# Earlier gathers in the inputs of layer 0 with the norm on ScalarE, 16384 bytes for descriptors, and a register read one tile ahead

## What is computed

```python
def mixture(x):                       # per token: the two best experts of the gate
    w = softmax(top2(x @ Wg + bg + bias))
    return sum(w[k] * (relu(x @ W1[e[k]] + b1[e[k]]) @ W2[e[k]] + b2[e[k]]) for k in (0, 1))

x = x + mixture(layernorm(x))         # its sum is taken in the attention inputs of layer 0
h = layernorm(x)
q, k, v = rope(h @ Wq + bq), rope(h @ Wk + bk), h @ Wv + bv
```

## Time and profile before

| | us |
|---|---|
| median of three runs | 2529.16 (2523.53 to 2530.19) |
| the profiled execution | 2531.16, its span 2529.3 |
| expert tiles, layer 0 | about 451 to 568 |
| attention inputs, layer 0 | about 570 to 720 |
| attention inputs, layer 1 | about 1403 to 1480 |
| expert tiles, layer 1 | about 2277 to 2412 |
| closing stage | about 2412 to 2529 |

### The profile page before, as it was taken

The page is one execution under the profiler, slowest core; times in us unless marked ns, Lnnn a source line. Parts: engine busy times, 40 slices in busy tenths (PEclk is TensorE's granted clock), DMA queues, the critical chain, the costliest instruction groups (busy, mean ns, idle before and its releaser), DMA issues. The chain is left out here.

```text
span 2529.3 us, 45491 instructions
## 1 busy us (share of the span) xinstructions
PE 2030.4 (80%) x16896; PEld 958.9 (38%) x16896; DVE 1988.9 (79%) x3319; ACT 1507.4 (60%) x2948; POOL 593.3 (23%) x702
## 2 busy tenths in 40 slices
PE   6999675882479999999999579999999999369910
PEld 4888464771222222222222322222222222359910
DVE  7887647565679999999994779999999994576635
ACT  5553330340118988989888218988989889105500
POOL 2444300667520000000000340000000000316555
PEclk9999885895769999999999769999999999559955
DMA  5000010243341010110100351010110100302211
GB/s 192 1 1 1 0 32 11 78 91 78 115 147 32 20 42 19 33 42 20 42 6 10 110 153 31 21 42 19 32 42 20 42 6 10 122 10 74 64 51 55
DMA packets 94411, 121.16 MB, mean 48 GB/s; under 512 B 23664, under 2 KB 56560, under 8 KB 93936
## 3 DMA queue, kind: packets, MB, share of 16 engines
q1 hardware_dynamic: 73712, 78.92, 11.3%
q0 software_dynamic: 8960, 18.37, 3.0%
q10 hardware_dynamic: 11520, 20.98, 2.7%
HBM read 69.70 MB, written 42.99 MB: 45 GB/s over the span
## 5 line engine op out<-in xcount | busy, mean ns | idle before, releaser
L1489 DVE TENSOR_REDUCE mx<-psum 128x1 f32<-128x1024 f32 x1024 | 1175.1, 1216 | 82.2 <-PE psum L1377 81.3
L1466 ACT ACTIVATE p<-psum 128x512 f32<-128x512 f32 x2048 | 1102.5, 596 | 108.8 <-PE psum L1399 66.2
L1411 PE MATMUL psum<-p,v_ext 128*32 128x256 f32 x8192 | 656.5, 392 | 39.3 <-ACT p L1466 39.2
L1377 PE MATMUL psum<-ks,qs 64*128 64x512 bf16 x2048 | 636.0, 395 | 53.1 <-DVE mx L1489 29.9
L1399 PE MATMUL psum<-qs,ks 64*128 64x512 bf16 x2048 | 630.6, 383 | 1.5 <-ACT p L1466 1.3
L1411 PEld LDWEIGHTS psum<-p,v_ext 128*32 128x32 f32 x8192 | 162.2, 108 | 474.2 <-ACT p L1466 254.6
L1279 POOL CAST m_near<-mx 128x16 bf16<-128x16 f32 x128 | 25.1, 196 | 1080.9 <-DVE mx L1489 1076.8
L1399 PEld LDWEIGHTS psum<-qs,ks 64*128 64x128 bf16 x2048 | 123.4, 93 | 404.0 <-ACT p L1466 368.0
L746 ACT ACTIVATE hid<-psum,stage 128x128 f32<-128x128 f32 x448 | 132.1, 366 | 180.3 <-PE psum L716 180.3
L690 POOL DMA_INDIRECT x_in<-n_rows,token_of x152 | 166.2, 1093 | 296.3 <-POOLq L85 229.2
L1377 PEld LDWEIGHTS psum<-ks,qs 64*128 64x128 bf16 x2048 | 118.7, 94 | 115.3 <-DVE mx L1489 81.3
(11 more groups left out here) (229 smaller groups left out, 2120.7 us busy)
## 6 DMA issues: line engine op xcount, KB each, us to landing
qs<-qk_parts SPq DMA_DIRECT2D x128, 104.0 KB
ks<-qk_parts SPq DMA_DIRECT2D x128, 104.0 KB
qk_parts<-piece__1 ACTq DMA_DIRECT2D x40, 256.0 KB, 3.7
qk_parts<-piece__2 ACTq DMA_DIRECT2D x40, 256.0 KB, 3.5
answers<-y_out SPq DMA_DIRECT2D x152, 64.0 KB, 1.5
ew<-in_moe SPq DMA_DIRECT2D x1, 5136.0 KB, 18.8
ew<-in_moe SPq DMA_DIRECT2D x1, 4624.0 KB, 13.9
n_rows<-n_all SPq DMA_DIRECT2D x8, 512.0 KB, 3.2
```

The costliest lines, as they stand in the source:

```text
L1377: pe.matmul(psum[:, bank, :], a["qs"][r, g % NKF, j % KM, i * P:(i + 1) * P], a["ks"][r, g % NKF, j % KM, k * HALF:(k + 1) * HALF], start= ...
L1411: last = pe.matmul(psum[GR * j:GR * j + VW, O_BANK, q], t["v_ext"][:, b * NT + i, VE * (h0 + j):VE * (h0 + j) + VW], a["p"][:, (GH * s + j ...
L1466: act.activation(a["p"][:, n % NP, :], psum[:, S_BANK + n % NS, :], ACT.Exp, scale=DH ** -0.5)\
L1489: dve.tensor_reduce(a["mx"][:, g % 2, h, j, 0, c:c + 1], psum[:, bank:bank + 2, :].rearrange("p a c -> p (a c)"), AX.X, ALU.max)\
```

## The change

Four things. In the attention inputs of layer 0, batch 1 is normalised after batch 0 has been rotated; GpSimd issues all 64 gathers first, each batch behind the wait for its place, and the rests of batches 0 and 1 move to VectorE, each one job behind its rotation. In the attention inputs of both layers the eight tile operations of the norm move from VectorE to ScalarE, which applies x times rstd plus a shift; VectorE computes the shift in one small operation. The memory for descriptors is 16384 bytes. In the expert tiles of both layers the register with the expert's number is read one tile ahead, behind the stage copy before.

```diff
@@ expert_tiles, VectorE
-            def stage_weights(i):
-                e = dve.value_load(t["expert_of"][0:1, i:i + 1], min_val=0, max_val=t["E"] - 1)
+            def find_expert(i):
+                return dve.value_load(t["expert_of"][0:1, i:i + 1], min_val=0, max_val=t["E"] - 1)
+
+            def stage_weights(i, e):
                 if i >= NST:
                     dve.wait_ge(y_ready, i - NST + 1)
                 dve.tensor_copy(t["stage"][:, i % NST, :], t["ew"][:, bass.ds(e, 1), :]
                                 .rearrange("p a c -> p (a c)")).then_inc(staged, 1)
-            stage_weights(0)
+            stage_weights(0, find_expert(0))
+            e = find_expert(1)
             for i in range(tiles + 2):
...
                 if i + 1 < tiles:
-                    stage_weights(i + 1)
+                    stage_weights(i + 1, e)
+                    if i + 2 < tiles:
+                        e = find_expert(i + 2)
@@ attention_inputs
+    def after(b):
+        return layer == 0 and b == 1
+
+    def rested_by_vector(b):
+        return layer == 0 and b < 2
@@ TensorE
-                if b + 1 < B:
+                if b + 1 < B and not after(b + 1):
                     turn(b + 1)
                 project(b, (1,))
                 values(b)
+                if after(b + 1):
+                    turn(b + 1)
+        def take_rest(eng, n):
...
+            eng.wait_ge(piece0, n + 1)
+            if n >= RESTS:
+                eng.wait_ge(piece2, n - RESTS + 1)
+            eng.tensor_tensor(a["rest"][:, n % RESTS, :], a["rot"][:, n % ROTS, :],
+                              a["pieces"][0][:, pair % PAIRS, c], ALU.subtract).then_inc(rest, 1)
@@ VectorE, norm(b)
-                norm_steps(dve, t, link, (var_ready, std_ready, tile_ready), b, a["x"][b](), a["norm"][b]())
...
+                dve.scalar_tensor_tensor(t["shift"][:, 0, :], t["mv"][:, :, 0], -1.0, rstd, ALU.mult, ALU.mult)\
+                    .then_inc(scales_ready, 1)
@@ VectorE, rotate(b)
+                    if rested_by_vector(b) and n > JB * b:
+                        take_rest(dve, n - 1)
                     if layer == 0 and n >= LATE:
                         last_piece(dve, n - LATE)
...
+                if rested_by_vector(b):
+                    take_rest(dve, JB * (b + 1) - 1)
...
-                if b + 1 < B:
+                if b + 1 < B and not after(b + 1):
                     norm(b + 1)
                 rotate(b)
+                if after(b + 1):
+                    norm(b + 1)
@@ GpSimd
             if layer == 0:
-                for b in range(2):
+                for b in range(B):
+                    if b >= 2:
+                        pool.wait_ge(mixed, 2 * NT * (b - 1))
                     fetch(pool, t, b)
-            for b in range(B):
-                if layer == 0 and b + 2 < B:
-                    pool.wait_ge(mixed, 2 * NT * (b + 1))
-                    fetch(pool, t, b + 2)
-                take_rest(b)
+            for n in range(len(jobs)):
+                if not rested_by_vector(n // JB):
+                    take_rest(pool, n)
+                if layer and n >= LATE:
+                    last_piece(pool, n - LATE)
@@ ScalarE, copy_turned(b), behind the root
+                act.wait_ge(scales_ready, b + 1)
+                for i in range(NT):
+                    act.activation(a["norm"][b](i, 1).rearrange("p a d -> p (a d)"),
+                                   a["x"][b](i, 1).rearrange("p a d -> p (a d)"), ACT.Identity,
+                                   scale=t["rstd"][:, 0, i:i + 1], bias=t["shift"][:, 0, i:i + 1]).then_inc(tile_ready, 1)
@@ ScalarE, the order of batches
-                if b + 1 < B:
+                if b + 1 < B and not after(b + 1):
                     copy_turned(b + 1)
                 for n in range(JB * b, JB * (b + 1)):
                     first_piece(n)
-                    if n:
+                    if n and not (n == JB and after(1)):
                         second_piece(n - 1)
+                if after(b + 1):
+                    second_piece(JB * (b + 1) - 1)
+                    copy_turned(b + 1)
@@ kernel
-    nc = bacc.Bacc("TRN2", target_bir_lowering=False, num_devices=1, dynamic_dma_scratch_size=2048)
+    nc = bacc.Bacc("TRN2", target_bir_lowering=False, num_devices=1, dynamic_dma_scratch_size=16384)
```

More of the change, by code:

```diff
@@ L997, in attention_inputs @@
     T_BANK, V_BANK = 6, 4
-    with stage(nc, "loaded", "row_set", "rows_stored", "mixed", "step", "var_ready", "std_ready", "tile_ready", "turned",
+    def after(b):
+        return layer == 0 and b == 1
+    def rested_by_vector(b):
+        return layer == 0 and b < 2
+    with stage(nc, "loaded", "row_set", "rows_stored", "mixed", "step", "var_ready", "std_ready", "scales_ready", "tile_ready", "turned",
                "y_copied", "proj_done", "rot_a", "rot_used", "summed", "piece0", "rest", "piece1", "piece2", "v_done", "v_used", "cleared") as \
-            (block, loaded, row_set, rows_stored, mixed, step, var_ready, std_ready, tile_ready, turned,
+            (block, loaded, row_set, rows_stored, mixed, step, var_ready, std_ready, scales_ready, tile_ready, turned,
              y_copied, proj_done, rot_a, rot_used, summed, piece0, rest, piece1, piece2, v_done, v_used, cleared):
@@ L1071, in _ @@
                 values(b)
+                if after(b + 1):
+                    turn(b + 1)
+        def take_rest(eng, n):
+            b, k, h = jobs[n]
+            c, pair = slice(h * HALF, (h + 1) * HALF), 2 * b + k
+            eng.wait_ge(piece0, n + 1)
[3 more added lines that the diff above has]
+                              a["pieces"][0][:, pair % PAIRS, c], ALU.subtract).then_inc(rest, 1)
         def last_piece(eng, n):
@@ L1087, in norm @@
                     combine(dve, t, b, mixed, a["x"][b], a["x"][b], 2 * NT * b)
-                norm_steps(dve, t, link, (var_ready, std_ready, tile_ready), b, a["x"][b](), a["norm"][b]())
+                var, std, rstd, tmp = (t[k][:, 0, :] for k in ("var", "std", "rstd", "tmp"))
+                for i in range(NT):
+                    last = dve.bn_stats(t["stats"][:, i, :], a["x"][b](i, 1).rearrange("p a d -> p (a d)"))
+                link(last)
+                for i in range(NT):
+                    last = dve.bn_aggr(t["mv"][:, i, :], t["stats"][:, i, :])
+                link(last)
+                dve.tensor_scalar(var, t["mv"][:, :, 1], EPS, None, ALU.add).then_inc(var_ready, 1)
+                dve.wait_ge(std_ready, b + 1)
+                link(dve.reciprocal(rstd, std))
+                link(dve.tensor_tensor(tmp, rstd, rstd, ALU.mult))
+                link(dve.tensor_tensor(tmp, tmp, var, ALU.mult))
+                link(dve.tensor_scalar(tmp, tmp, -0.5, 1.5, ALU.mult, ALU.add))
+                link(dve.tensor_tensor(rstd, rstd, tmp, ALU.mult))
+                dve.scalar_tensor_tensor(t["shift"][:, 0, :], t["mv"][:, :, 0], -1.0, rstd, ALU.mult, ALU.mult)\
+                    .then_inc(scales_ready, 1)
             def rotate(b):
@@ L1139, in _ @@
         def _(pool):
-            def take_rest(b):
-                for n in range(JB * b, JB * (b + 1)):
-                    _, k, h = jobs[n]
-                    c, pair = slice(h * HALF, (h + 1) * HALF), 2 * b + k
-                    pool.wait_ge(piece0, n + 1)
-                    if n >= RESTS:
-                        pool.wait_ge(piece2, n - RESTS + 1)
-                    pool.tensor_tensor(a["rest"][:, n % RESTS, :], a["rot"][:, n % ROTS, :],
-                                       a["pieces"][0][:, pair % PAIRS, c], ALU.subtract).then_inc(rest, 1)
-                    if layer and n >= LATE:
-                        last_piece(pool, n - LATE)
             if layer == 0:
-                for b in range(2):
+                for b in range(B):
+                    if b >= 2:
+                        pool.wait_ge(mixed, 2 * NT * (b - 1))
                     fetch(pool, t, b)
-            for b in range(B):
-                if layer == 0 and b + 2 < B:
-                    pool.wait_ge(mixed, 2 * NT * (b + 1))
-                    fetch(pool, t, b + 2)
-                take_rest(b)
+            for n in range(len(jobs)):
[3 more added lines that the diff above has]
+                    last_piece(pool, n - LATE)
             if layer:
```

## The result

The changed kernel takes 2498.39 us (median of 4 runs, 2496.07 to 2502.17) against 2529.64 for the kernel before: a ratio of 0.9886, 95% interval 0.9873 to 0.9898, or -31 us. Forecast were 2495.2 in a range of 2485 to 2510.

The account below looks back on a forecast made before the run. Bounds were seen in GpSimd's gathers, stalled by descriptor room and order, and VectorE's register load in layer-0 tiles; -7.5 - 17 - 8 - 0.5 - 1 = -34 us gave 2495.2, range 2485 to 2510.

Parts of the forecast that it names:

- Closing stage, -7.5: Closing stage: with more descriptor room, four holes between the 64 gathers, together 7.5 us, go; 0 if they have another cause.
- 112 gathers: Descriptor room: if 2048 bytes hold 14 gathers, 16384 hold some 112, more than the run of 64.
- Layer-0 inputs, -17: Attention inputs of layer 0: with the new order the last combine starts at 662.5, not 679.40, so -17 us.
- Rival D: Layer-0 inputs: VectorE's two-operand work holds nearly every gather, +35 us, 2564 in all; chance 0.04.
- Layer-0 tiles, -8: Expert tiles of layer 0: the early register read brings a tile to 1.30 us, so -8 us.
- if x waits for it, 0.34 comes back: 2.6, 1.30: Layer-0 tiles: if the moved read holds the next x copy, two tiles take 2.6 us, 1.30 each.
- rival C: Layer-0 tiles: the load's idle time only moves, tiles stay at 1.35; -26 us in all, 2503; chance 0.10.
- 2.5 landing + 3.4 pipeline: End of layer-0 tiles: time added behind the last gather's start, 550.1, to put the stage's end at 556.0.
- at 1.35: Layer-0 tiles: the case of 1.35 us a tile, put at -3.6 us.
- Layer-1 tiles, -0.5: Expert tiles of layer 1: VectorE's idle time is hidden behind TensorE's 1.91 us rhythm; -0.5 us, from 0 to -1.5.
- Layer-1 inputs, -1: Attention inputs of layer 1: norm moved from VectorE to ScalarE, which has no slack left; -1 us, from -3 to +2.
- Full blocking: Layer-0 inputs: VectorE's two-operand work holds gathers at full length, 15 us; last combine at 671, only -8.5.

Follow-up runs that it names:

- e2: The kernel before with 4096 bytes for descriptors in place of 2048, nothing else; ratio to before 1.0002.
- e6: The changed kernel without the register reads of both expert tile stages, expert taken from the tile number; ratio to before 0.9867.
- e12: The changed kernel with each expert number read just ahead of its stage copy again; ratio to before 0.9901.
- e1: The kernel before with 16384 bytes for descriptors in place of 2048, nothing else; ratio to before 0.9995, on a chip of the 2555 kind.

## Why the prediction held, and where it did not

**Closing stage, -7.5: right**, size and place. "No issue over 0.3" stands in the profile, and a batch of 16 gathers with the holds under its combination takes 22.8 as forecast. What carried it was the view: the holes ended where landing times ended. The "112 gathers" that I gave to 16384 bytes was a proportion that e2 contradicts. It cost nothing here, since 64 fit either way.

**Layer-0 inputs, -17: right, -18.7.** The last combination came 20.2 us earlier (88.6 for 108.8), and the way behind it, which was to stay, grew by 1.5. Counted from the first gather, the steps came at: scales 29.5 (forecast 29.6), rotation 35.6 (34.4), combination 1 49.8 (48.4), combination 2 65.2 (67.0), last combination 88.6 (91.9). Two sizes were off, both on the safe side. Two-operand work beside gathers cost about 2 us in place of my 5: the gathers beside it took 1.15 to 1.45 in place of 0.94, and most took 0.94. So the last landing came at 88.6 in place of 91.9. VectorE's path (forecast 90.9) came to the same 88.6, and neither set the end alone. Rival D falls with this. The Trainium skill's rule that a VectorE instruction with two SBUF inputs holds a GpSimd one that reads SBUF ("SBUF — State Buffer", section "Who interferes with whom") shows as at most 0.5 us on a gather in this stage, apart from the second half of a combination, which gives the 1.65 us again (593.78). Beside a longer instruction it shows more: in the closing stage a gather begun at 2418.82, 0.06 us into an addition of 1.22 us (L965), took 1.98.

**Layer-0 tiles, -8: wrong, +0.5 and +1.1.** Two steps failed. The first is "if x waits for it, 0.34 comes back: 2.6, 1.30". I took the 0.44 that is gained ahead of the stage copy and the 0.34 lost behind it from different bases. In the trace the instructions y and stage take nearly the same time from start to start, 0.42 and 0.41, so a read that holds the next instruction until 0.73 costs 0.31 or 0.32 behind either: nothing is won. That is rival C, to which I gave 0.10. The rate of 1.30 in place of 1.33 was worth only 2.4 us over 79 steps, though.

The larger part of the 8 us is the second step, "2.5 landing + 3.4 pipeline": 5.9 us from the start of the last gather to the end of the stage. The kernel before has 11.4 there (556.13 to 567.5), the changed one 11.1 and e6 11.4. So 5.5 us of the forecast were a gain over nothing, and even the case "at 1.35" came out at -3.6 although it is slower than the 1.33 of the kernel before. In e6 the last gather began at 549.64, as forecast for 1.25 (550.1), and the stage ended at 561.07 in place of 556.0.

**Layer-1 tiles, -0.5: too small, -2.6 to -3.4.** I read the rhythm of 1.91 from two neighbouring loads. Over 71 steps it was 1.95 before and is 1.92 now. Idle time on VectorE that I called hidden was not quite so; e12, which puts the read back, has 149.5.

**Layer-1 inputs, -1: right in size** (-1.2 between the averages of eight and six profiles), though one profile cannot tell it. The forecast of ScalarE as the next bound holds in part. Its wait for the rotation (12.4 us in all before) is gone, and ahead of first pieces it now spends its time on DMA issues of its own, but it still waits 11.7 us for GpSimd's rests.

**Sum.** What repeats is -18 in layer 0's inputs, -7.5 in the closing stage, -3 in layer 1's tiles, -1.2 in its inputs, +0.8 in layer 0's tiles: -28.9, against -31.2 and -29.6 by the medians of the two measurements. The forecast of -34 was within 3 to 4.5 us because the 8 us that failed were partly made up by terms that I had set too small; that much of the agreement is luck. Rival C's 2503 was too slow for the same reason.

**Slips in the working that changed no verdict.** VectorE's path to the last combination is worked out as 661.5, which is -18, and then used as 660.5, -19. Full blocking by the terms given ends at 672.5, -7, and not at 671, -8.5. From the last gather's landing to the end of the kernel are 17.6 us (2511.7 to 2529.3), more than the 15 stated, and still less than the 22.8 of a batch.

What the prediction could not see is the other kind of chip. On it the room alone gives nothing, and what the changed kernel gives there was not measured.

## To carry to other kernels

An idle gap ahead of an instruction is not a gain until the next order is written out engine by engine: take start-to-start distances of each instruction in the loop and put the moved cost behind its new neighbour; only a neighbour longer than the cost hides it. A register read cost VectorE 0.64 us in each place tried here, less what the instruction ahead of it covered, and two reads didn't hide one another. When a rate is turned into the end of a stage, take the time behind the last transfer from the trace too: 11.4 us here, not the 5.9 of an undisturbed landing and pipeline. Read a rhythm over the whole loop rather than from two rows, and ask of a bound that is lifted what its slack had been covering.

## What was not expected of the hardware

- Doubling 2048 bytes for descriptors removed every hole between 64 gathers of 128 rows (closing stage 94.8 to 95.2 us with 2048, 87.3 with 4096, 87.2 with 16384).
- The same program takes 2530 us on some chips and 2555 on two others. On the slower ones VectorE, ScalarE and GpSimd stand still together in the tiles (5.62, 2.97 and 2.23 us at 470 in e1), and the other tiles of layer 0 take about 1.5 us in place of 1.36. VectorE stands still 14 to 19 us in layer 0's inputs once the gathers run without holes. The trace names no releaser.
- Two register reads in a row hold VectorE's next instruction until 1.37 us after the start of the one ahead of them, one read until 0.73.
- Gathers of layer 0's tiles that land 2.7 us behind their start at 540 take 7.6 at 556, when other transfers fill the queues (before; 7.3 in the changed kernel).
